# Expert tiles of two sizes in the routed feed-forward stage: 25 of 256 rows and 21 of 128 rows

## The reference, cut to what matters

```python
logits = x @ gate_w + gate_b
top_w, top_idx = top_k(softmax(logits), 2)      # 2 of 8 experts for each token
combine[t, top_idx[t]] = top_w[t] / sum(top_w[t])
h     = silu(x @ w1[e]) * (x @ w3[e])           # 128 -> 512, for each expert e
out_e = h @ w2[e]                               # 512 -> 128
out   = sum over e of out_e * combine[:, e]
x     = x + layernorm(out)
```

## Time and profile before

| | us |
|---|---|
| median of 3 runs | 1280.5 (1279.04 to 1280.61) |
| the profiled execution | 1280.58 |
| its span, first to last instruction | 1278.8 |
| index chain, 997.4 to 1033.6 | 36 |
| expert loop, first turned tile to start of last scatter, 1032.9 to 1241.2 | 208 |
| from there to the end of the span | 37.6 |

### The profile page before, as it was taken

One profiled execution on the slowest core, in us unless ns is written; L12 is line 12 of the kernel. 1 busy time (PEld: TensorE's weight loads), 2 busy tenths in 40 slices (PEclk: granted clock), 3 DMA queues, 4 the chain that ended last, 5 costly groups with the idle time before them and its releaser, 6 DMA issues. The chain is left out here.

```text
span 1278.8 us, 16507 instructions
## 1 busy us (share of the span) xinstructions
PE 1082.7 (85%) x4934; PEld 547.4 (43%) x4934; DVE 955.2 (75%) x1181; ACT 748.4 (59%) x1306; POOL 730.6 (57%) x640
## 2 busy tenths in 40 slices
PE   7876799999999987888989898989898388887853
PEld 3322244444444433333334333333335277776753
DVE  4898585665755439999999999999991876565545
ACT  6586545655556255767767686857653345454445
POOL 0222261431513005899898989897983167777764
PEclk8898899999999998999999999999998589999986
DMA  7000000000000003222322222222210111111225
GB/s 232 1 0 0 1 1 1 1 1 1 1 1 1 1 0 109 100 83 93 98 84 88 86 84 92 70 69 77 73 58 9 58 36 50 51 54 51 50 58 182
DMA packets 33966, 67.21 MB, mean 53 GB/s; under 512 B 7168, under 2 KB 7360, under 8 KB 33664
## 3 DMA queue, kind: packets, MB, share of 16 engines
q1 hardware_dynamic: 28464, 55.23, 13.4%
q0 software_dynamic: 4992, 10.23, 3.0%
q10 hardware_dynamic: 432, 0.76, 0.2%
HBM read 56.63 MB, written 9.57 MB: 52 GB/s over the span
## 5 line engine op out<-in xcount | busy, mean ns | idle before, releaser
L1936 POOL TENSOR_TENSOR prod<-hs,csb 128x1024 f32<-128x1024 f32 x128 | 301.9, 2359 | 125.3 <-DVE hs L1982 120.0
L1982 DVE TENSOR_TENSOR_SCAN hs<-dA,first,pD 128x1024 f32<-128x1024 f32 x128 | 300.4, 2347 | 5.2 <-DVE pD L1995 0.8
L1664 PE MATMUL pY<-prod,const 128*128 128x512 f32 x512 | 241.5, 597 | 5.0 <-POOL prod L1936 5.0
L1809 ACT ACTIVATE dA<-dt,negA 128x511 f32<-128x511 f32 x256 | 169.4, 712 | 1.5 <-DVE dt L2037 1.4
L1995 DVE TENSOR_TENSOR pD<-dtu,pD 128x1024 f32<-128x1024 f32 x128 | 154.9, 1211 | 10.0 <-ACT pD L1824 9.7
L1664 PEld LDWEIGHTS pY<-prod,const 128*128 128x128 f32 x512 | 97.5, 192 | 109.9 <-issue 92.2
L2471 POOL DMA_INDIRECT g<-moe_rows,source x78 | 82.4, 1056 | 55.5 <-DVE source L2666 26.7
L2717 DVE SCALAR_TENSOR_TENSOR hid<-pR,silu 128x512 f32<-128x512 f32 x78 | 53.9, 692 | 67.2 <-ACT silu L2425 67.2
L1162 ACT ACTIVATE stage<-pR,vec 128x512 f32<-128x512 f32 x64 | 43.9, 687 | 99.7 <-PE pR L891 99.5
L2490 POOL DMA_INDIRECT moe_outs<-y,to x78 | 81.1, 1039 | 26.2 <-issue 22.8
L1824 ACT ACTIVATE pD<-first 128x1 f32<-128x1 f32 x128 | 21.6, 169 | 119.4 <-PE pD L1674 98.2
(11 more groups left out here) (477 smaller groups left out, 2588.1 us busy)
## 6 DMA issues: line engine op xcount, KB each, us to landing
csb<-ssm_c SPq DMA_DIRECT2D x128, 256.0 KB, 3.1
raw<-moe_w SPq DMA_DIRECT2D x12, 512.0 KB, 4.8
room<-moe_outs SPq DMA_DIRECT2D x8, 512.0 KB, 8.3
hidw<-hid_w SPq DMA_DIRECT2D x1, 2048.0 KB, 10.0
moe_rows<-xt SPq DMA_DIRECT2D x8, 256.0 KB, 2.0
outT<-X SPq DMA_DIRECT2D x8, 256.0 KB, 2.0
X<-xT SPq DMA_DIRECT2D x3, 512.0 KB, 4.1
g<-moe_rows,source POOLq DMA_INDIRECT x78, 2.6
```

Of the source, the lines that this page charges most:

```text
L1664: last = nc.tensor.matmul(YB[c][:], G.ident, prod[:, slot(b, n), c, :], start=n == 0, stop=n == DST - 1)
L1809: last = nc.scalar.activation(dA[:, slot(b, n), c, 1:N], dt[:, b, c, 1:N], ACT.Exp, scale=negA[:, c, n:n + 1])
L1936: nc.gpsimd.tensor_tensor(prod[:, slot(b, n), :, :], hs[:, slot(b, n), :, :], csb[:, slot(b, n), :, :].to_broadcast([P, CB, N]), ALU.mult)\
L1982: nc.vector.tensor_tensor_scan(hs[:, slot(b, n), :, :].rearrange("p c n -> p (c n)"), dA[:, slot(b, n), :, :].rearrange("p c n -> p (c n)" ...
```

## The change

The tiles come in two sizes. An expert with c pairs gets floor(c / 256) full tiles and, for the rest, one or two half tiles of 128 slots. The code is unrolled for 25 full tiles (`FULL`, the fewest there can be) followed by 21 half tiles; full tiles of an expert beyond the 25th are done as two half tiles each. So there are 46 tiles and 71 columns (`COLS`), where there were 39 and 78. A half tile has one gather and one scatter, half the columns in `x_turn`, `up`, `silu`, `hid`, `hid_high`, `hid_low_part`, `take_x` and `put_y`, and half the matmuls in `down` and `x_turn`. `up` has as many matmuls as before, over 128 columns. The index chain gets longer: slots of full tiles and of half tiles are placed apart, and the expert of a tile is found from its first column. `parts(i)` is 2 for a full tile and 1 for a half tile.

```diff
-    TILES = (PAIRS * P + E * (ROWS - 1)) // ROWS
-    COLS = 2 * TILES
+    FULL = -(-(PAIRS * P - E * (ROWS - 1)) // ROWS)
+    COLS = (PAIRS * P + E * (P - 1)) // P
+    TILES = FULL + COLS - 2 * FULL
...
+        def parts(i):
+            return 2 if i < FULL else 1
+        def first_column(i):
+            return 2 * i if i < FULL else FULL + i
+        def halves(w, i):
+            return w if i < FULL else w.rearrange("p (h s) -> p h s", h=2)[:, :, 0:P]
...
-                    for r in range(2):
+                    for r in range(parts(i)):
...
-                        last = product(out[:, u, h * ROWS:(h + 1) * ROWS], of_expert(w13_hi, e, m), of_expert(w13_lo, e, m),
-                                       x16[:, i % 2, 0, :], x16[:, i % 2, 1, :], True, True)
+                        rows_ = parts(i) * P
+                        last = product(out[:, u, h * ROWS:h * ROWS + rows_], of_expert(w13_hi, e, m), of_expert(w13_lo, e, m),
+                                       x16[:, i % 2, 0, 0:rows_], x16[:, i % 2, 1, 0:rows_], True, True)
...
-                    for r in range(2):
+                    for r in range(parts(i)):
                         out = Y[:, i % 2, r * P:(r + 1) * P]
...
-                nc.scalar.activation(hid_hi[:, n % HR, :], hid[:, n % HR, :], ACT.Copy).then_inc(S["hid_high"], 1)
+                nc.scalar.activation(halves(hid_hi[:, n % HR, :], n // 2), halves(hid[:, n % HR, :], n // 2), ACT.Copy).then_inc(S["hid_high"], 1)
...
+            nc.gpsimd.iota(column_i[:, 0:FULL], [[2, FULL]], base=0, channel_multiplier=0)
+            nc.gpsimd.iota(column_i[:, FULL:], [[1, TILES - FULL]], base=2 * FULL, channel_multiplier=0)
...
-                for r in range(2):
+                for r in range(parts(i)):
+                    c = first_column(i) + r
...
-            nc.vector.scalar_tensor_tensor(out=grid[:, :, :], in0=steps, scalar=float(ROWS),
-                                           in1=counts.unsqueeze(2).to_broadcast([P, E, GRID]),
...
+            nc.vector.scalar_tensor_tensor(out=full_grid[:, :, :], in0=per_expert(lane_f[:, 1:GRID // 2 + 1], GRID // 2),
+                                           scalar=float(ROWS), in1=counts.unsqueeze(2).to_broadcast([P, E, GRID // 2]),
+                                           op0=ALU.mult, op1=ALU.is_le).then_inc(S["grid"], 1)
...
+            nc.vector.scalar_tensor_tensor(out=left[:, :, :], in0=left[:, :, :], scalar=float(P),
+                                           in1=jump[:, :].unsqueeze(2).to_broadcast([P, E, CHUNKS]),
+                                           op0=ALU.mult, op1=ALU.mult).then_inc(S["left"], 1)
...
+            nc.vector.tensor_tensor(past[:, :, :], limits[:, :, :].rearrange("p k e -> p (k e)").unsqueeze(1)
+                                    .to_broadcast([1, TILES, 2 * E]),
+                                    column_f[:, :].unsqueeze(2).to_broadcast([1, TILES, 2 * E]), ALU.is_le)\
```

More of the change, by code:

```diff
@@ L2111, in phase_moe @@
         grid = sb("grid4", [P, E, GRID])
-        tiles_of = sb("tiles_of4", [P, E])
-        tiles_to = sb("tiles_to4", [P, E])
-        tiles_from = sb("tiles_from4", [P, E])
+        halves_of = sb("halves_of4", [P, E])
+        full_of = sb("full_of4", [P, E])
+        full_to = sb("full_to4", [P, E])
+        full_from = sb("full_from4", [P, E])
+        halves_to = sb("halves_to4", [P, E])
+        both = sb("both4", [P, E])
+        jump = sb("jump4", [P, E])
+        full_grid = sb("full_grid4", [P, E, GRID // 2])
+        left = sb("left4", [P, E, CHUNKS])
+        limits = sb("limits4", [1, 2, E])
+        column_i = sb("column_i4", [1, TILES], I32)
+        column_f = sb("column_f4", [1, TILES])
         one8 = sb("one8_4", [P, E])
@@ L2122, in phase_moe @@
         low_h = sb("low_h4", [P, PAIRS], F16)
-        past = sb("past4", [1, TILES, E])
+        past = sb("past4", [1, TILES, 2 * E])
         expert_f = sb("expert_f4", [1, TILES])
@@ L2178, in tile_of, with moved @@
             return i % B, ds(i // B)
+        def parts(i):
+            return 2 if i < FULL else 1
+        def first_column(i):
+            return 2 * i if i < FULL else FULL + i
+        def moved(i, places):
+            return 16 * sum(parts(j) for j in range(i % places, i + 1, places))
+        def halves(w, i):
+            return w if i < FULL else w.rearrange("p (h s) -> p h s", h=2)[:, :, 0:P]
         def slab(i):
@@ L2194, in _ @@
             for r in range(YR):
-                sp.wait_ge(S[f"scattered{r}"], 32 * len(range(r, TILES, YR)))
+                sp.wait_ge(S[f"scattered{r}"], 16 * sum(parts(j) for j in range(r, TILES, YR)))
             by_pair = outs[0:P * PAIRS, :].rearrange("(p k c) d -> p k c d", k=2, c=CHUNKS)
@@ L2281, in x_turn @@
             def x_turn(i):
-                pe.wait_ge(S[f"gathered{i % GR}"], 32 * (i // GR + 1))
+                pe.wait_ge(S[f"gathered{i % GR}"], moved(i, GR))
                 if i >= 2:
@@ L2322, in down @@
                         last = nc.tensor.matmul(out, hid_lo[:, n % HR, at], w_hi,
-                                                start=False, stop=u == 1 and h == 1 and r == 1)
+                                                start=False, stop=u == 1 and h == 1 and r == parts(i) - 1)
                 last.then_inc(S["down"], 1)
@@ L2424, in _ @@
                     act.wait_ge(S["hidden"], n - 1)
-                nc.scalar.activation(silu[:, u, :], R1[:, u, :], ACT.Silu, scale=1.0 / WS).then_inc(S["silus"], 1)
+                nc.scalar.activation(halves(silu[:, u, :], i), halves(R1[:, u, :], i), ACT.Silu, scale=1.0 / WS).then_inc(S["silus"], 1)
                 if n >= 1:
@@ L2488, in _ @@
                 pool.wait_ge(S["y_out"], i + 1)
-                for r in range(2):
+                for r in range(parts(i)):
+                    c = first_column(i) + r
                     nc.gpsimd.indirect_dma_start(
-                        outs, bass.IndirectOffsetOnAxis(ap=to[:, 2 * i + r:2 * i + r + 1], axis=0),
+                        outs, bass.IndirectOffsetOnAxis(ap=to[:, c:c + 1], axis=0),
                         y[:, i % YR, r, :], None).then_inc(S[f"scattered{i % YR}"], 16)
@@ L2601, in _, with per_expert @@
[L2601 to L2607, removed]
-            dve.wait_ge(S["ranked"], 1)
-            nc.vector.scalar_tensor_tensor(out=place[:, :, :], in0=tiles_from[:, :].unsqueeze(2).to_broadcast([P, E, CHUNKS]),
+            def per_expert(steps, n):
+                return steps.unsqueeze(1).to_broadcast([P, E, n])
@@ new lines, in _ @@
+            dve.wait_ge(S["full_to"], 1)
+            nc.vector.tensor_tensor(full_from[:, :], full_to[:, :], full_of[:, :], ALU.subtract).then_inc(S["full_from"], 1)
+            dve.wait_ge(S["halves_of"], 2)
+            nc.vector.tensor_tensor_scan(halves_to[:, :], one8[:, :], halves_of[:, :], 0.0, ALU.mult, ALU.add)\
+              .then_inc(S["halves_to"], 1)
+            nc.vector.tensor_scalar(both[:, :], full_to[:, :], full_to[:, E - 1:E], 2.0, ALU.subtract, ALU.mult)\
+              .then_inc(S["both"], 1)
@@ L2610, in _ @@
+            dve.wait_ge(S["halves_to"], 1)
+            nc.vector.tensor_tensor(jump[:, :], halves_to[:, :], halves_of[:, :], ALU.subtract).then_inc(S["jump"], 1)
+            dve.wait_ge(S["full_from"], 1)
+            nc.vector.scalar_tensor_tensor(out=place[:, :, :], in0=full_from[:, :].unsqueeze(2).to_broadcast([P, E, CHUNKS]),
                                            scalar=float(ROWS), in1=rank, op0=ALU.mult, op1=ALU.add)\
               .then_inc(S["place"], 1)
+            dve.wait_ge(S["both"], 1)
@@ L2612, in _ @@
+            dve.wait_ge(S["left"], 2)
             dve.wait_ge(S["place"], 1)
+            nc.vector.tensor_tensor(place[:, :, :], place[:, :, :], left[:, :, :], ALU.add).then_inc(S["place"], 1)
+            dve.wait_ge(S["place"], 2)
             nc.vector.tensor_tensor(placed[:, :, :, :], picks[:, :, :, :],
@@ L2690, in _ @@
             dve.wait_ge(S["expert_f"], 1)
+            nc.vector.scalar_tensor_tensor(out=expert_f[:, :], in0=past[:, :, E - 1], scalar=-float(E), in1=expert_f[:, :],
+                                           op0=ALU.mult, op1=ALU.add).then_inc(S["expert_f"], 1)
+            dve.wait_ge(S["expert_f"], 2)
             nc.vector.tensor_scalar(expert[:, :], expert_f[:, :], float(E - 1), None, ALU.min).then_inc(S["expert"], 1)
@@ L2707, in hid_low_part @@
                     dve.wait_ge(S["down"], n - HR + 1)
-                nc.vector.tensor_tensor(hid_lo[:, n % HR, :], hid[:, n % HR, :], hid_hi[:, n % HR, :], ALU.subtract)\
+                low, whole, high = (halves(w[:, n % HR, :], n // 2) for w in (hid_lo, hid, hid_hi))
+                nc.vector.tensor_tensor(low, whole, high, ALU.subtract)\
                   .then_inc(S["hid_low"], 1)
@@ L2716, in _ @@
                     dve.wait_ge(S["hid_low"], n - HR + 1)
-                nc.vector.scalar_tensor_tensor(out=hid[:, n % HR, :], in0=R3[:, u, :], scalar=1.0 / WS,
```

(3 more changed lines are left out.)

42 lines of the change are left out of this document (29 added, 13 removed).

## The result

The changed kernel takes 1286.5 us (median of 8 runs, 1283.7 to 1290.1) beside 1280.6 us of the kernel before on the same chip (8 runs, 1278.7 to 1281.9): a ratio of 1.0052, with a 95% interval of 1.0040 to 1.0064. So it is slower, by 5 to 8 us. The profiled execution took 1285.71 us with a span of 1283.9 us, 5.1 us more than the span of before.

The account below looks back on a forecast made before the run. POOL bounds full tiles at 5.33 us, PE's sequencer half tiles at 3.9. Start and chain +2.8 and loop +6.0 move the last turn +8.8; the drain gives back 4.7: 1280.6 + 4.1 = 1284.7 us, range 1276 to 1291.5.

Parts of the forecast that it names:

- The index chain: DVE instructions ahead of PE's first turn: 5 become 15, tables and sums change size; `expert` +2.5 us later.
- The start: Two more iotas on POOL and a DVE cast ahead of the router's constants: +0.3 us (0 to 0.4).
- The full tiles: Expert loop's full tiles run as before, 2.8 us later; turn of tile 25 at 1156.8, of tile 30 at 1176.8.
- The half tiles: Loop from tile 30: sequencer sets 3.9 us each (3.6 to 4.1), 15 take 58.5 us, last turn at 1235.3.
- The drain: Last turn to last scatter: 9.9 us instead of 14.6, last scatter at 1245.2.
- What follows: Everything after the last scatter: unchanged.
- The sequencer keeps up: Half tiles: steps speed up, under 3.6 us a tile, POOL's 2.67 us pace holds; 1264.5 us; chance 0.15.
- The clock falls: Half tiles: array's clock drops to 0.50, 4.2 us a tile from tile 25; +10, 1291 us; chance 0.12.
- Nothing much: Whole kernel: a chain 1.5 us less and half tiles of 3.8 us give +1.5; same overall 0.19.
- What would show it: Profile signs: loads 3.9 us apart, POOL waiting for `y_out`, PE busy towards 60%, `expert` 2.5 to 2.8 later, last scatter near 1245.

Follow-up runs that it names:

- the steps taken away: Changed kernel with the 21 half tiles addressing expert 0's weights by constants, number still loaded and checked: 1265.1 us, ratio 0.989.
- the extra load: Expert number loaded a second time, unused, for each half tile of the changed kernel: 1302.1 us; in the last 21 tiles of the kernel before: 1278.8 us.
- the bound check: Changed kernel with expert numbers loaded without the check that they lie within the experts: 1281.2 us, ratio 1.0015.
- its six variants: Changed kernel with constant addresses 1265.1 us, second load 1302.1, no check 1281.2, `up` over 64 columns 1286.9, half and full tiles in turn 1267.3, that without check 1268.0.
- its two variants: Kernel before with a second expert-number load in its last 21 tiles, 1278.8 us, and with the longer index chain's added DVE instructions alone, 1283.7 us.
- the run with 64 columns: Changed kernel with `up` in the half tiles over 64 columns instead of 128, half their rows not computed: 1286.9 us, ratio 1.0053.
- the alternating order: Changed kernel with 8 full tiles, then half and full in turn 17 times, then 4 half tiles: 1267.3 us, ratio 0.989.

## Why the prediction was right

Forecast: 1284.7 us, by the sequencer at 3.9 us a half tile. Measured: 1286.5, slower by 5 to 8 us where +4.1 was forecast. The mechanism is the one the prediction names, shown by the steps taken away (loads at POOL's 2.69 us), by the extra load that costs its length in one kernel and nothing in the other, and by the bound check. Term by term, by the profiled execution:

*The index chain* was put at +2.5 us at `expert` and is +2.5.

```profile
1004.84 0.29 DVE L2625 SCALAR_TENSOR_TENSOR full_grid<-lane_f,pR 128x128 f32<-128x128 f32 x1 [0.29 <-PE pR L2283]
...
1008.36 0.69 DVE L2668 TENSOR_TENSOR placed<-picks,place 128x512 f32<-128x512 f32 x1
...
1034.07 0.18 DVE L2754 TENSOR_SCALAR expert<-expert_f 1x46 int32<-1x46 f32 x1
```

From the grid to `placed` it takes 3.52 us and took 1.50, +2.0 where +2.1 was forecast; from there to `expert` 25.71 and took 25.20, +0.5 where +0.4 was.

*The start*, +0.3 forecast, can't be seen: the first expert number is loaded at 1034.29, 2.3 us later than in before, but the layer itself began 1.5 us later in this execution, in code that is the same, and the router's part took 1.7 us less. Both are larger than the term.

*The full tiles*: the turn of tile 25 came at 1157.38, forecast 1156.8, and that of tile 30 at 1178.29, forecast 1176.8.

*The half tiles* are the term that was mis-sized: 15 x 4.06 = 60.9 us instead of 15 x 3.9 = 58.5. The last turn:

```profile
1239.14 0.27 PE L2309 MATMUL pX<-ident,g 128*128 128x128 f16 x2 [0.60 <-issue]
```

It is 3.8 us behind the forecast of 1235.3: 0.6 from the full tiles, 0.9 from the five tiles after them and 2.4 from these fifteen. The 3.9 was the distance of a single pair of loads, taken as a figure for all, and that tile is short of one instruction: the wait for `y_out` is written only from the third tile's `down` on. It is L2313 in the kernel before and L2336 in the changed one (above), and it first comes at 1049.7, behind the pair of loads at 1043.5 and 1047.4:

```profile
L2313 PEldq EVENT_SEMAPHORE  x37: 51/51/51, 1049.7 to 1233.4; - x37
```

A wait that is met still takes 0.11 us from its start to the next instruction's. Start to start, the tile of 3.91 us has 0.65 us for the load and its check, 0.23 for two waits (with the issue of the turn) and 3.03 for the 24 steps; the fifteen half tiles have on average 0.69, 0.36 for three waits and 3.01, which makes 4.06. So the steps are as fast with a half tile's matmuls behind them as with a full tile's, as forecast, and what was missed is the third wait, 0.12 us, and 0.04 at the load. The earlier trace rows hide some of it in another way: 0.6 and 3.3 us leave out the whole second from 1101.7 to 1102.7, also the 0.1 that a wait takes when it is met; with that, the tile takes 4.0 us. The measured 4.06 lies within the bounds of 3.6 to 4.1.

*The drain*: from the last turn to the last scatter 9.8 us, forecast 9.9. So the last scatter is at 1248.9 and not at 1245.2.

*What follows* was put at unchanged and wasn't: from the last scatter's start to the end of the span 35.0 us instead of 37.6. The SP timeline of after, and the landing of its reads by the list of DMA issues:

```profile
1251.24 5.72 SPq L2220 DMA_DIRECT2D room<-moe_outs  x8
```

The eight reads are issued within 5.7 us (6.5 before) and land after 7.6 us in the median (8.3 before), and the rest of the stage is shorter too. In the profiles the changed kernel and its six variants have 34.6 to 35.3 us here, the kernel before and its two variants 36.1 to 37.6. Why is open; no experiment was made on it. So that the profiled execution's 1285.7 us is within 1.0 us of the sum is luck, of two misses that offset each other: +3.7 up to the last scatter, -2.6 behind it.

*The rivals.* "The sequencer keeps up" fell: its condition, a half tile under 3.6 us, isn't met by the changed kernel, and the run with constants shows the time that it would have given (1265.1, the rival's figure 1264.5). "The clock falls" fell for this kernel, with 1.00 in the half tiles, and its price fell with it: at 0.55 in the run with 64 columns nothing was lost. That run has less work for the array than the rival supposed, so what the clock would cost with the full 128 columns stays open; the extra load brought it to 0.87 and 0.83 there, with tiles of 4.75 us, of which the load accounts for all but 0.04. "Nothing much" is excluded by the interval of 5 to 8 us. Its sum had a slip: a chain of 1.5 us less and fifteen half tiles of 3.8 us take 3.0 from the 4.1 and leave +1.1, not +1.5.

*What would show it* came in part. The loads are evenly spaced, at 4.06 us and not 3.9; `x_turn` doesn't wait for DMA there; the "issue" entries and the clock of 1.00 are there. POOL waits, but the view names PE's products (`pR` L2232, 11 times) and not `y_out` as what ended last, up to the last six scatters (the kernel lets POOL wait for `up` too, before each gather); and the kernel before already had two waits for `y_out`, of 1.4 and 1.7 us, among its last six scatters. The `expert` instruction comes 2.3 us later (1034.07 against 1031.80) and not 2.5 to 2.8, and the last scatter comes at 1248.9 and not near 1245. PE busy doesn't fall towards 60%, it reads 33.6 of 40 us. A matmul's modelled duration of 0.22 us covers the gap to the next one at 0.12, so PE looks 84% busy where its columns fill 38 x 0.056 = 2.1 of 4.06 us.

## What to carry to other kernels

A tile whose weights are chosen by a register cost the sequencer one step for each slice of weights, whatever the number of columns: before tiles are made smaller, count steps, loads and waits, also those that will be met, and compare their sum with the engine that is to be relieved. Take the sum from a tile in the middle of the loop; the first ones can lack a wait. Cutting the work of one engine helps only to where the next is; two kinds of tiles with different bounds cost the sum of both bounds if they run one kind after the other (5.33 + 4.06 us here), and the bound of the pair if they alternate (8.06). Look for an instruction queue as the bound wherever no engine rises when the old bound falls.

## What the runs showed of the hardware

- The 24 register steps of a tile take PE's sequencer the same time with 256 or 128 columns in the matmuls (3.03 and 3.01 us), and the whole tile with a granted clock of 1.00 or 0.55 (4.06 and 4.03 us). The load of a register from SBUF costs 0.65 us with its bound check, 0.3 of it the check; a wait that is met costs 0.11 us.
- The granted clock can fall to 0.55 and the time stay the same, when the array isn't what sets the pace (1286.9 us beside 1286.5, with `up` over 64 columns).
- From the start of the layer to the first load of an expert number it took 55.2 to 62.7 us in the ten profiled executions, with no order by what was changed (55.7 before, 56.5 after, 62.7 in the alternating order and with the extra load in after, 59.7 with it in before). So a profiled execution's own time is good for a sum within the loop, but not to 1 us for the whole, and the sum of a few microseconds has to be read at the loop's own ends.
